# Three of eight context batches transposed by VectorE's 32x32 blocks instead of by TensorE, with K tiles made of every eighth column

## The reference: what is computed

```python
# x, ctx: (8, 256, 1024) float32; all weights 1024 x 1024
def attn(text, features, Wq, bq, Wk, bk):
    Q = einsum('btx,dx->btd', text, Wq) + bq
    K = einsum('bpx,dx->bpd', features, Wk) + bk
    scores = einsum('btd,bpd->btp', Q, K) / sqrt(1024)
    return einsum('btp,bpd->btd', softmax(scores), features)

x = x + attn(layernorm(x), ctx, Wq, bq, Wk, bk)
# ffn: weights = scales * ((4-bit w > 0 ? 1 : -1) - zeros), then x @ weights + bias
x = x + ffn(layernorm(x))
```

## Time and profile before

| | |
|---|---|
| median of 3 runs | 555.62 us (555.33 to 556.01) |
| profiled execution | 555.69 us, span 553.9 us |
| TensorE (PE) busy | 98% of the span |
| VectorE (DVE) busy | 70% |
| ScalarE (ACT) busy | 43% |
| GpSimd (POOL) busy | 34% |
| TensorE's granted clock | full over the whole span |

### The profile page before, as it was taken

One profiled execution on the slowest core, in us unless ns is written; L12 is line 12 of the kernel. 1 busy time (PEld: TensorE's weight loads), 2 busy tenths in 40 slices (PEclk: granted clock), 3 DMA queues, 4 the chain that ended last, 5 costly groups with the idle time before them and its releaser, 6 DMA issues.

```text
span 553.9 us, 7445 instructions
## 1 busy us (share of the span) xinstructions
PE 545.2 (98%) x2702; PEld 456.5 (82%) x2702; DVE 385.4 (70%) x643; ACT 239.1 (43%) x426; POOL 186.0 (34%) x143
## 2 busy tenths in 40 slices
PE   7999999999999999999999999999999999999997
PEld 6888888887777877878889999999788888888886
DVE  4977776689899997794213555574777788778742
ACT  6964354301431341242337766676473253234210
POOL 2072000000000000000125977777667545743630
PEclk9999999999999999999999999999999999999999
DMA  8842100349677855743335699898527776773411
GB/s 286 260 158 72 38 1 0 113 153 316 202 208 262 230 191 165 216 166 146 143 124 219 239 354 352 322 402 318 216 77 227 229 222 233 212 243 111 120 76 76
DMA packets 47187, 106.59 MB, mean 192 GB/s; under 512 B 3576, under 2 KB 24064, under 8 KB 44976
## 3 DMA queue, kind: packets, MB, share of 16 engines
q1 hardware_dynamic: 40624, 99.84, 51.5%
q10 hardware_dynamic: 6528, 6.29, 5.5%
HBM read 66.27 MB, written 39.85 MB: 192 GB/s over the span
## 4 chain that ended last, share of the span: by engine, by line
PE 76%; DVE 11%; DMA 5%; ACT 4%; issue 2%; POOL 1%; SPq 0%; ACTq 0%; DVEq 0%; POOLq 0%
PE bank L1236 19%; PE bank L1238 18%; PE bank L1237 18%; PE bank L1280 5%; PE bank L1283 5%; PE bank L1286 5%; DVE junk L1002 2%; PE bank L1338 2%; DMA xq<-xn_scratch 2%; DVE stats L912 1%; DVE xT_lo L854 1%; DMA wk_stage<-in_L_xattn_Wk 1%; DMA right_scratch<-part_hi 1%; DVE xin L942 1%; DMA xn_scratch<-xin 1%
## 5 line engine op out<-in xcount | busy, mean ns | idle before, releaser
L1236 PE MATMUL bank<-xT_hi,m_hi 128*128 128x512 f32 x256 | 103.4, 404 | 0.4 <-DVE xT_lo L854 0.4
L1237 PE MATMUL bank<-xT_lo,m_hi 128*128 128x512 f32 x256 | 99.8, 390 | 0.0
L1238 PE MATMUL bank<-xT_hi,m_lo 128*128 128x512 f32 x256 | 99.7, 390 | 0.0
L746 ACT ACTIVATE t_pair<-bank,ucol 128x512 f32<-128x512 f32 x32 | 21.9, 686 | 105.2 <-PE bank L1238 105.2
L1188 DVE TENSOR_TENSOR xres<-xres,bank 128x512 f32<-128x512 f32 x56 | 38.2, 681 | 36.3 <-PE bank L1238 36.1
L545 POOL TENSOR_TENSOR tT_lo<-t_pair,tT_hi 128x1024 fp32r<-128x1024 f32 x16 | 38.1, 2401 | 75.0 <-ACT tT_hi L587 75.0
L524 POOL TENSOR_TENSOR pairs<-mv,pairs 128x2 f32<-128x2 f32 x8 | 5.5, 693 | 161.3 <-DVE mv L921 161.3
L559 POOL TENSOR_TENSOR l_lo_s<-l_sum_s,l_hi_s 128x512 fp32r<-128x512 f32 x32 | 40.4, 1294 | 56.0 <-DVE l_sum_s L1129 56.0
L1236 PEld LDWEIGHTS bank<-xT_hi,m_hi 128*128 128x128 f32 x256 | 48.1, 188 | 12.2 <-DVE xT_lo L854 0.8
L1238 PEld LDWEIGHTS bank<-xT_hi,m_lo 128*128 128x128 f32 x256 | 48.1, 188 | 10.1
L1237 PEld LDWEIGHTS bank<-xT_lo,m_hi 128*128 128x128 f32 x256 | 48.2, 188 | 9.9 <-issue 0.2
(11 more groups left out here) (148 smaller groups left out, 1256.2 us busy)
## 6 DMA issues: line engine op xcount, KB each, us to landing
cin<-in_ctx SPq DMA_DIRECT2D x8, 1024.0 KB, 5.5
xres<-in_x SPq DMA_DIRECT2D x8, 1024.0 KB, 11.4
out<-xres SPq DMA_DIRECT2D x15, 512.0 KB, 5.8
right_scratch<-part_hi SPq DMA_DIRECT2D x28, 256.0 KB, 2.2
xn_scratch<-xin SPq DMA_DIRECT2D x6, 1024.0 KB, 4.9
xq<-xn_scratch ACTq DMA_DIRECT2D x24, 256.0 KB, 5.8
r_tile<-right_scratch SPq DMA_DIRECT2D x6, 1024.0 KB, 11.3
yn_scratch<-yin SPq DMA_DIRECT2D x6, 1024.0 KB, 4.4
```

The costliest lines, as they stand in the source:

```text
L1236: pe.matmul(out_, a_hi, b_hi, start=start, stop=False, skip_group_check=True)
L1237: pe.matmul(out_, a_hi, b_lo, start=False, stop=False, skip_group_check=True)
L1238: return pe.matmul(out_, a_lo, b_hi, start=False, stop=stop, skip_group_check=True)
```

## The change

For batches 0, 1 and 2 (`BLOCKS = 3`), `c_tr` is gone from TensorE. SyncE loads the rows of ctx by quadrant (`load_quadrants_of_ctx`: four transfers, each 32 partitions x 8 x 256 elements), and VectorE transposes 32x32 blocks straight into the PSUM bank (`c_blocks`, four for each batch). Such a tile k holds columns k, k + 8, k + 16, ... of ctx. The other operand has to be in the same order, so `m_hi` and `m_lo` are written tile by tile, from a PSUM bank that is read at every eighth element; `u_sums` takes every eighth element of `uacc` as the stationary operand; and the transposes that TensorE keeps (batches 3 to 7) take every eighth column of `cin`. The plain rows of batches 0 to 2, which `ctx_hi` and `cn_lo` need, are loaded by themselves once the blocks are done: the buffers are the same.

```diff
+BLOCKS = 3
+        def by_tile(cols):
+            return cols.rearrange("q (p k) -> q k p", k=NB)
+        def by_tile_of_m(m, b, n):
+            return m[:, b, :].rearrange("q (k p) -> q k p", k=NB)[:, :, P // 2 * n:P // 2 * (n + 1)]
+        def bank_of_m(b, n):
+            return by_tile(m_bank(b, n)[:, :])
...
+            def load_quadrants_of_ctx(b):
+                if b == 0:
+                    sp.wait_ge(s_xlo, NB * PAIRS)
+                elif b == 1:
+                    for name in R_SUM:
+                        sp.wait_ge(s_lst[name], 16 * KH)
+                else:
+                    sp.wait_ge(s_t, NB * PAIRS)
+                rows = ctx[b].rearrange("(m j) f -> j m f", j=32)
+                for a in range(4):
+                    sp.dma_start(cq[b][32 * a:32 * a + 32, :, :], rows[:, :, a * S:(a + 1) * S]).then_inc(s_cql[b], 16)
             def load_ctx(b):
+                if b < BLOCKS:
+                    sp.wait_ge(s_cb, 4 * b + 4)
...
-                    copy(m_hi[:, b, n * HALF:(n + 1) * HALF], m_bank(b, n)[:, :]).then_inc(s_mhi, 1)
+                    copy(by_tile_of_m(m_hi, b, n), bank_of_m(b, n)).then_inc(s_mhi, 1)
...
-                    low(m_lo[:, b, cols], m_bank(b, n)[:, :], m_hi[:, b, cols], s_mlo)
+                    low(by_tile_of_m(m_lo, b, n), bank_of_m(b, n), by_tile_of_m(m_hi, b, n), s_mlo)
...
+            def c_blocks(b, u):
+                if u == 0:
+                    dve.wait_ge(s_cql[b], 64)
+                    if b == 1:
+                        dve.wait_ge(s_tev, NB * PAIRS)
+                if b > 1 or u > 1:
+                    dve.wait_ge(s_clo, 4 * b + u - 1)
+                dve.transpose(c_bank(b, u)[:, :].rearrange("p (k m j) -> p m k j", k=2, m=NB),
+                              cq[b].rearrange("p m (i k) -> p m k i", k=NB)[:, :, 2 * u:2 * u + 2, :]).then_inc(s_cb, 1)
...
-                    pe.matmul(bank[4][:, 2 * j:2 * j + 2], uacc[:, j * P:(j + 1) * P], ones2, start=True, stop=True)
+                    pe.matmul(bank[4][:, 2 * j:2 * j + 2], by_tile(uacc)[:, j, :], ones2, start=True, stop=True)
...
-                        o, f = i * S + t * P, (2 * u + i) * P
-                        ins = pe.transpose(c_bank(b, u)[:, o:o + P], cin[b % 3][:, t, f:f + P], ident)
+                        o = i * S + t * P
+                        ins = pe.transpose(c_bank(b, u)[:, o:o + P], by_tile(cin[b % 3][:, t, :])[:, 2 * u + i, :], ident)
```

More of the change, by code:

```diff
@@ L162, in xattn_ffn_kernel @@
         cin = [at(f"cin{i}", kb, [P, QT, D], F32) for i, kb in enumerate((162.25, 170.25, 57.75))]
+        cq = [at(f"cq{b}", kb, [P, NB, S], F32) for b, kb in enumerate((162.25, 170.25, 57.75))]
         xres = [at(f"xres{b}", slot[b], [P, QT, D], F32) for b in range(B)]
@@ L219, in xattn_ffn_kernel @@
         s_cl = [sem(f"ctx_loaded{i}") for i in range(3)]
+        s_cql = [sem(f"ctx{b}_by_quadrant_loaded") for b in range(BLOCKS)]
+        s_cb = sem("ctx_transposed_by_blocks")
         s_ctr, s_chi, s_clo = sem("ctx_transposed"), sem("cT_hi_done"), sem("cT_lo_done")
@@ L358, in _ @@
                     sp.dma_start(xin[:, 1, :, :], x_rows[1]).then_inc(s_xl[1], 16)
-            def load_ctx(b):
[L361 to L367, removed]
+            def load_quadrants_of_ctx(b):
[4 more added lines that the diff above has]
+                        sp.wait_ge(s_lst[name], 16 * KH)
+                else:
+                    sp.wait_ge(s_t, NB * PAIRS)
+                rows = ctx[b].rearrange("(m j) f -> j m f", j=32)
+                for a in range(4):
+                    sp.dma_start(cq[b][32 * a:32 * a + 32, :, :], rows[:, :, a * S:(a + 1) * S]).then_inc(s_cql[b], 16)
+            def load_ctx(b):
+                if b < BLOCKS:
+                    sp.wait_ge(s_cb, 4 * b + 4)
                 else:
                     sp.wait_ge(s_cnlo, 4 * (b - 2))
-                    sp.wait_ge(s_ctr, 4 * (b - 2))
+                    if b >= 3 + BLOCKS:
+                        sp.wait_ge(s_ctr, 4 * (b - 2 - BLOCKS))
                 sp.dma_start(cin[b % 3], ctx_rows[b]).then_inc(s_cl[b % 3], 16)
@@ L439, in _ @@
                 sp.wait_ge(s_lst[name], 16 * KH)
-            load_ctx(2)
+            load_ctx(0)
+            load_quadrants_of_ctx(2)
+            load_ctx(1)
             load_right(0, 0, 3)
@@ L680, in c_hi @@
                     act.wait_ge(s_dot, B)
-                elif b > 1:
+                elif b == 1:
+                    act.wait_ge(s_t, NB * PAIRS)
+                else:
                     act.wait_ge(s_sc, NB * (b - 1) + 2 * u + 2)
@@ L1079, in _ @@
                         x_blocks(X_BLOCKS[n])
+                    if p == PAIRS - 1 and j == 5:
+                        c_blocks(0, 0)
+                        c_blocks(0, 1)
                     if p == PAIRS - 1 and j == 6:
                         c_lo(0, 0)
+                        c_blocks(0, 2)
                         c_lo(0, 1)
+                        c_blocks(0, 3)
                 if p < PAIRS - 1:
@@ L1153, in _ @@
                     invert_sum(b - 1)
-                if b + 1 < B:
+                if b + 1 < BLOCKS:
+                    c_blocks(b + 1, 0)
+                    c_blocks(b + 1, 1)
                     c_lo(b + 1, 0)
+                    c_blocks(b + 1, 2)
                     c_lo(b + 1, 1)
+                    c_blocks(b + 1, 3)
                     if b == 1:
@@ L1161, in _ @@
                     c_lo(b + 1, 3)
+                elif b + 1 < B:
+                    for u in range(4):
+                        c_lo(b + 1, u)
                 else:
@@ L1360, in _ @@
                             gather(GATHER[n - h], h)
-                    if p == PAIRS - 1 and j in (5, 7):
-                        for u in (j - 5, j - 4):
-                            c_tr(0, u)
             def p_tr(b):
```

27 lines of the change are left out of this document (12 added, 15 removed).

## The result

The changed kernel takes **564.11 us** in the median of 6 runs (562.07 to 564.69), beside 555.48 us (554.92 to 556.01, 6 runs) of the kernel before: a ratio of 1.0149, 95% interval 1.0137 to 1.0160. It is slower by 8.6 us, where 12.5 us were forecast.

What follows compares the result with a forecast made beforehand. The prediction took TensorE's queue as the bound, except where it stands still. Its terms 1.4 + 8.4 + 1.7 + 1.0 = 12.5 us on the profiled 555.69 us gave 568.1 us, range 556.2 to 570.5.

Steps and rivals of the forecast that it cites:

- The transposes removed, and the blocks on VectorE: Batches 0 to 2: 5.2 us of TensorE's queue gone, 7.6 us lost to waits on VectorE's blocks; net +1.4 us.
- Waits of 0.6, 2.0 and 5.0 us: TensorE waiting in scores(1) for its c_lo, ahead of p_tr(0) for batch 0's softmax, ahead of pv(0) for p_lo(0).
- The strided weight loads: The 80 transposes left on TensorE, called bound by weight load: 0.105 us more per load, +8.4 us.
- u_sums: Its 16 matmuls load uacc at every eighth element: 0.105 us more each, +1.7 us.
- m_hi and m_lo: Strided PSUM reads ahead of wrow, taken at twice the reading time: +1.0 us on the chain.
- The factor of two: Reads at every eighth element take twice as long, taken from ScalarE's 1236 and 2469 ns and VectorE's block transposes.
- DMA: Three MB more loaded, xres(0) asked for later: nothing taken, 1 us kept for the range.
- The rival of the clock: Gap ahead of pv(0) brings TensorE to 1.2 GHz: at most 5.5 us more, 573 us; chance 0.05.
- the first case: Rival that strided reads are free: only the 1.4 us stay, 557.0 us, from 556.2 to 558.5; chance 0.27.

## Why the prediction was right or wrong

**The transposes removed, and the blocks on VectorE (+1.4 us): right.** Waits of 0.6, 2.0 and 5.0 us were laid out; 0.17, 1.81 and 4.54 came, and the net loss was 1.4 us at `pv(0)`. That the total came out to the tenth is partly luck. The measured waits are 6.5 us where 7.6 were laid out; and the forecast takes off 1.0 us or so for waits of before, where the trace has one wait of 0.43 us. By the waits alone the loss would be 6.5 - 0.4 - 5.2 = 0.9 us; 0.1 us more is the wait for `wt` in stage 2 (0.85 us against 0.71), 0.1 us is a gap of TensorE between 298 and 299 us (busy 0.86 of 1.00 us), and the last 0.3 us stay open. The cause of the longest wait was shown by moving `p_lo(0)` ahead of two blocks, which took off 2.5 us.

**The strided weight loads (+8.4 us): this step failed.** 0.2 us were measured. The sentence was that these transposes are bound by the weight load, and the evidence for it was `u_sums`. But `u_sums` consists of plain fp32 passes, and these load otherwise than transposes do. Groups of eight strided transposes last 1.05 us instead of 1.03, which is 0.2 us over all 80; the kernel with 128 of them and no blocks shows 276 ns each, against 274. The price of a strided load itself, twice the contiguous one, was right wherever a plain fp32 matmul does it: 0.105 to 0.224 us in `u_sums`, and 0.13 us more per pass against the identity.

**u_sums (+1.7 us): right, 1.9.** What it led to was missed: the granted clock fell to 0.50 in each of the four profiles in which slow loads (at 16 or 32 bytes) stand in one piece, between 1.5 us before the end of the row and 1 us behind it, and near 100 us in no other. That cost 3.1 us in the profiled execution, more than the loads.

**m_hi and m_lo (+1.0 us): wrong, nothing.** The factor of two came from rows in which SBUF is read. Of these, ScalarE's pair differs in the stride alone; VectorE's two block transposes (1150 and 577 ns) also differ in size and in where they write, and no run separates that. Reading PSUM at the same stride is free for both engines (590 and 677 ns). The Trainium skill, page Advanced Engine Details and Errata, section PSUM Cachelines, warns of gaps for matmuls; no run here has TensorE write at a stride, and for these reads the rows show no cost.

**DMA (0 to 1 us): right, nothing.** `xres(0)` was not waited for in the changed kernel, since `pv(0)` itself was late. It came to be waited for, 0.5 us, in the kernel with two batches by blocks.

**The rival of the clock was given too little.** It was tied to the gap ahead of `pv(0)` and did come there, but at 2.0 us, not 5.5, and together with the slow loads of `u_sums`, not instead of them. The rival is also added up in two ways: 573 us is 5.5 us on top of the forecast of 568.1 (573.6, strictly), while on top of the first case, as its heading says, it would be 557.0 + 5.5 = 562.5 us, inside the range. In the profiles with two waits there of 1.8 us and of 2.05 or 4.54 us the clock fell near `pv(0)` each time (five kernels); with waits of 0.6 and 1.1 us or less it did not. No run has such waits without the rest of the change, so that they are the cause is argued, not shown. Two of six runs had a higher mean clock (0.994 against 0.988 to 0.991) and were 2 us faster.

So of the 12.5 us forecast 8.2 + 1.0 didn't come, and 5.1 us of clock in two places came that weren't in the sum, with 0.2 us more for `u_sums` and 0.4 us that I can't place: 9.0 us. The total of 568.1 us was 4.0 us above the median, nearer than its terms were, since the errors went both ways.

## What to carry to other kernels

Ask of a strided stationary operand which kind of pass loads it, and whether the passes stand in one row: with fp32 at 16 or 32 bytes a plain pass pays double, a transpose next to nothing, and an instruction upstream that writes the operand in order takes the price away. A row of slow loads can cost more by the clock behind it than by itself, so look at the granted clock as well as at the busy time. Work that goes from the bound engine to an idle one is worth what it takes only where it doesn't stand between two links of a chain: the same two batches by blocks were 0.20% slower where they stood ahead of the softmax, and with half of one batch in idle time and the load of `xres` first 0.33% faster.

## What the runs showed of the hardware

- In a row of two-column matmuls, an fp32 load of 128 columns takes 0.105 us contiguously, 0.111 at 8 bytes, 0.219 at 16 bytes and 0.224 at 32 bytes. The loads at 16 bytes take no longer at a granted clock of 0.50 than at 1.00.
- An fp32 transpose with the same stride of 32 bytes goes from 274 to 276 ns in the mean of its records, a plain pass of 128 columns from 275 to 400 ns.
- TensorE's clock fell while the profile marks it as busy without a gap, during or behind 3.5 us of two-column matmuls with slow loads. With the same loads and 128 columns each, in the strided plain passes, the mean over the span stayed at 1.00.
- The clock was down for 3 to 7 us, and not equally in executions of one kernel: the kernel with only the order changed took from 557.74 us at a mean clock of 1.000 to 560.36 at 0.994.
- ScalarE and VectorE read PSUM at every eighth fp32 element as fast as contiguously.
